# Second routed FFN of a macaron block: two token groups, rows scattered into expert slabs, 62 tiles instead of 47

## The chip, the cores and the metric

One core of a Trainium2 chip. The metric is the device time of one execution, in microseconds (us); the kernel before has a median of 578.79 us over 3 runs (578.08 to 579.34). The engines are TensorE (PE; its weight loads are shown as PEld), VectorE (DVE), ScalarE (ACT), GpSimd (POOL) and SyncE (SP), which only issues DMAs.

## The reference, cut to what matters

The input x has 4 batches of 512 tokens with 256 features (2048 tokens, 16 "token tiles" of 128).

```python
x = x + 0.5 * ffn(layernorm(x))        # FFN 1
x = x + attention(layernorm(x))        # 3 heads, per batch of 512 tokens
x = x + 0.5 * ffn(layernorm(x))        # FFN 2, the same weights

def ffn(x):                            # 16 experts, 2 per token, hidden size 128
    scores = sigmoid(x @ gate_w)
    selected = top_k(scores + expert_bias, 2)
    w = scores[selected] / sum(scores[selected])
    shared = (silu(x @ shared_gate) * (x @ shared_up)) @ shared_down
    routed = sum over the 2 experts e of w_e * ((silu(x @ G_e) * (x @ U_e)) @ D_e)
    return shared + routed
```

The attention is softmax(Q K^T / 16) V with the softmax over the query axis (each key's column is normalised), a mean over heads, an output product and a bias. All is float32; matrix products are done as three passes over values split in a high and a low part (`three_pass`).

## The kernel before, in words

Every engine has its own program, written out in Python in order; semaphores join them. The stages are: loading and splitting weights, with front 1 (layernorm, router, routing tables); FFN 1; attention; front 2; FFN 2; a tail with the shared expert and the combination.

**A routed FFN.** The 4096 (token, expert) pairs are sorted by expert. Each expert's rows start at a multiple of 128, so 4096/128 + 15 = 47 tiles of 128 rows always hold them (`SLOT_TILES`, `NI`). The routing part computes a slot for each pair (`choose`, `rank_tokens`, `slots`), then the inverse, a token number for each slot (`pick_tiles`, `pick_lanes`, `scale_tokens`, `index_tokens`), with which POOL gathers rows of normalised tokens from `xn_dram` by indirect DMA (`load`, L1580). The loop `ffn` (L518 PE, L851 ACT, L1300 DVE, L1694 SP) is a software pipeline of 47 + 4 steps: in step s PE transposes h of tile s-3 (L543), transposes the rows of tile s (L330), multiplies tile s-1 by gate and up weights and tile s-4 by the down weights (L324). ACT copies four results of PE a step (L862, L867, L878, L885), DVE makes the low parts and the product (L1307, L1311, L1316), SP stores the result in `y_dram` (L1703). PE reads the experts' weight addresses with one load of four registers per four tiles (L527).

**Attention** has 48 units (`units`: batch, head, key tile). Unit u computes scores, exponentials (ACT L979), their high and low part (ACT L988, POOL L1621), values (ACT L991, DVE L1428), and the product `mix` of unit u-2. Beside the units run side pieces, one `next()` of a generator at a time: `side_pieces` (between mix and values on PE) and `side_pieces_late` (at the end of the unit). The generators prepare the next batch (`attn_front`) and the normalised rows and router of FFN 2 for the batch before (`previous_front`, `prev_front`), whose rows SP stores in `xn_dram` (L1673). Batch 3 steps its FFN 2 generator twice a unit from its 7th unit on.

**Front 2** is what remains after the last `mix`: measure and normalise batch 3, transposes for the shared expert (`front_turn` PE L376, `front_hi` ACT L768, `front_lo` DVE L1072; 8 pairs of token tiles), the router of batch 3, the choice, ranks, slots, the inverse. `stay_busy` puts products on PE that nobody reads.

**The tail** after the loop: the shared expert by batch (`shared_gu`, `shared_silu`, `shared_mul`, `shared_hi`, `shared_lo`, `shared_y`, `shared_sink`), beside 32 indirect gathers of result rows by POOL (L1545, two per token tile, in bursts of 8, each burst after the landing of the one before), which DVE adds to x (`combine`, L1238), and 16 output DMAs (L1726).

## Time and profile before

| | us |
|---|---|
| median of 3 runs | 578.79 |
| the profiled execution, whole | 576.65 |
| its span, to which all rows below refer | 575.4 |
| attention ends | 409.4 |
| first product of FFN 2's loop | 442.56 |
| last result copied out of the loop | 522.02 |

Busy shares of the span: PE 81%, PEld 71%, DVE 59%, ACT 47%, POOL 44%. The page's 40 slices are 14.4 us each; PE stands at 8 or 9 tenths in most slices from the 6th to the 36th, at 6 or 7 in 12, 13, 16, 29, 31 and 32, and falls to 7, 4, 3, 2 in the last four. The line PEclk under it is the clock that PE was granted; it is at 8 or 9 tenths but for 7 in slices 3 to 5, 31, 38 and 39 and 6 in the last.

### The profile page before, as it was taken

To read this page: it belongs to the slowest core of one execution; us is meant where nothing else is said; L and a number is where in the kernel's file an instruction comes from. 1 tells how busy PE (TensorE), PEld (TensorE's weight loads), DVE (VectorE), ACT (ScalarE), POOL (GpSimd) and SP (SyncE) were. 2 spreads that over 40 slices of the span, in tenths; PEclk is the share of its full clock that TensorE was granted. 3 is DMA by queue.
4 is the path that set the end of the run, shared out by engine and by line. 5 is a ranking of instruction groups with operands and counts; after the bars stand their busy time and mean duration, and the time that the engine had idled before them with its cause. 6 is when DMAs were issued, how large, how long until landed. Compare 5 with 4: busy or idle time off the path is not lost.

```text
span 575.4 us, 9851 instructions
## 1 busy us (share of the span) xinstructions
PE 465.3 (81%) x3029; PEld 408.9 (71%) x3029; DVE 337.1 (59%) x925; ACT 272.6 (47%) x740; POOL 253.8 (44%) x259
## 2 busy tenths in 40 slices
PE   1675599999867997999899988999786799997432
PEld 0344488888655996898789977999755789886321
DVE  5478665555284666377538763635766566663554
ACT  4758266666424444345344544447333666662010
POOL 5356765553152542363237321422204555534655
PEclk9977799999989999999899999999897999999776
DMA  8642356466321100020001100003011455562444
GB/s 302 238 129 92 110 183 179 149 202 147 105 61 59 47 1 0 21 65 27 1 19 56 38 2 1 9 29 111 1 36 49 136 167 161 168 140 92 128 132 133
DMA packets 37808, 53.61 MB, mean 93 GB/s; under 512 B 5568, under 2 KB 30528, under 8 KB 37760
## 3 DMA queue, kind: packets, MB, share of 16 engines
q1 hardware_dynamic: 29760, 32.25, 16.8%
q0 software_dynamic: 7584, 20.72, 14.0%
q8 instruction: 27, 0.44, 0.3%
q14 instruction: 21, 0.17, 0.1%
q10 hardware_dynamic: 416, 0.02, 0.0%
HBM read 34.37 MB, written 18.61 MB: 92 GB/s over the span
## 4 chain that ended last, share of the span: by engine, by line
PE 57%; DVE 16%; issue 9%; ACT 6%; DMA 5%; POOL 5%; another core or an unknown queue 0%; SPq 0%; ACTq 0%; POOLq 0%; DVEq 0%
PE bank L324 47%; POOL late_pair L1545 4%; PE bank L330 3%; PE bank L543 2%; DMA late_pair<-y_dram,slot_i 2%; DMA raw<-xn_dram,gather_at 2%; PE bank L489 2%; DVE x_sb L1297 1%; DVE softmax_row L1418 1%; DMA x_sb<-in_x 1%; DVE e_sp L1307 1%; PE bank L376 1%; DVE v_sp L1428 1%; ACT v_sp L991 1%; DVE pick_lane L1180 1%
## 5 line engine op out<-in xcount | busy, mean ns | idle before, releaser
L1580 POOL DMA_INDIRECT raw<-xn_dram,gather_at x94 | 90.4, 962 | 87.3 <-PE bank L330 37.2
L1621 POOL TENSOR_TENSOR e_sp<-raw,e_sp 128x512 fp32r<-128x512 f32 x48 | 62.7, 1307 | 127.8 <-ACT e_sp L988 127.6
L324 PEld LDWEIGHTS bank<-v_sp,e_sp 128*128 128x128 f32 x576 | 75.5, 193 | 3.2 <-POOL e_sp L1621 0.3
L324 PE MATMUL bank<-v_sp,e_sp 128*128 128x256 f32 x576 | 77.7, 285 | 0.0
L324 PE MATMUL bank<-g_sp,xT 128*128 128x512 f32 x288 | 75.7, 398 | 1.4 <-DVE g_sp L1323 1.4
L979 ACT ACTIVATE raw<-bank,softmax_row 128x512 f32<-128x512 f32 x48 | 33.2, 692 | 58.0 <-DVE softmax_row L1418 57.9
L324 PEld LDWEIGHTS bank<-g_sp,xT 128*128 128x128 f32 x288 | 52.1, 190 | 11.0 <-DVE g_sp L1323 1.8
L1418 DVE TENSOR_REDUCE softmax_row<-bank 128x1 f32<-128x512 f32 x48 | 32.9, 686 | 38.0 <-PE bank L324 37.7
L324 PE MATMUL bank<-w_hi,e_sp 128*128 x188 | 50.5, 292 | 0.6 <-DVE e_sp L1307 0.6
L1307 DVE TENSOR_TENSOR e_sp<-bank,e_sp 128x128 fp32r<-128x128 f32 x94 | 27.4, 291 | 39.3 <-ACT e_sp L862 33.2
L324 PE MATMUL bank<-w_hi,v_sp 128*128 128x256 f32 x64 | 20.4, 397 | 35.5 <-DVE v_sp L1084 30.0
L324 PE MATMUL bank<-b_sp,xT 128*128 128x256 f32 x288 | 43.9, 288 | 3.7 <-DVE v_sp L1428 3.5
L324 PE MATMUL bank<-w_hi,xT 128*128 x188 | 45.4, 304 | 1.6 <-DVE xT L1311 1.6
L324 PE MATMUL bank<-w_hi,xt_late 128*128 x188 | 45.4, 304 | 1.4 <-DVE xt_late L1311 1.2
L1428 DVE SCALAR_TENSOR_TENSOR v_sp<-bank,softmax_row,v_sp 128x256 fp32r<-128x256 f32 x48 | 23.2, 484 | 34.9 <-ACT v_sp L991 34.3
L1545 POOL DMA_INDIRECT late_pair<-y_dram,slot_i x32 | 30.3, 948 | 29.6 <-DMA y_dram<-stage 13.3
L330 PE MATMUL bank<-ident,raw 128*128 128x128 f32 x212 | 41.2, 276 | 2.7 <-DMA raw<-xn_dram,gather_at 2.5
L885 ACT COPY stage<-bank 128x256 f32<-128x256 f32 x94 | 35.6, 378 | 15.9 <-PE bank L324 11.2
L324 PEld LDWEIGHTS bank<-w_hi,v_sp 128*128 128x128 f32 x64 | 16.0, 289 | 38.0 <-DVE v_sp L1084 31.9
L878 ACT ACTIVATE raw<-bank 128x128 f32<-128x128 f32 x94 | 26.7, 284 | 34.1 <-PE bank L324 29.1
L324 PEld LDWEIGHTS bank<-b_sp,xT 128*128 128x128 f32 x288 | 38.1, 190 | 6.2 <-DVE v_sp L1428 5.3
L1537 POOL DMA_INDIRECT stage<-y_dram,slot_i x32 | 31.4, 980 | 22.7 <-DMA y_dram<-stage 14.9
(204 smaller groups left out, 1086.7 us busy)
## 6 DMA issues: line engine op xcount, KB each, us to landing
y_dram<-stage SPq DMA_DIRECT2D x94, 128.0 KB
xn_dram<-xn_all SPq DMA_DIRECT2D x5, 512.0 KB, 4.3
stage<-in_w_pack SPq DMA_DIRECT2D x6, 384.0 KB, 5.4
raw<-in_w_pack SPq DMA_DIRECT2D x6, 384.0 KB, 3.1
x_sb<-in_x SPq DMA_DIRECT2D x4, 512.0 KB, 7.7
out<-x_sb SPq DMA_DIRECT2D x16, 128.0 KB
stage_more<-in_w_pack SPq DMA_DIRECT2D x5, 384.0 KB, 3.4
xn_dram<-raw SPq DMA_DIRECT2D x12, 128.0 KB, 1.7
```

The lines of the kernel that those rows point to most:

```text
L324: m = pe.matmul(dst, lhs[k][l], rhs[k][r], start=(first and k == 0 and i == 0), stop=(last and k == n - 1 and i == 2), skip_group_check=True)
L330: m = pe.transpose(dst[:, k * P:(k + 1) * P], src[:, k * P:(k + 1) * P], ident[:])
L878: act.activation(h_buf[:, g % 2, :], bank[GU_BANKS[g % 2]][:, 0:F], ACT.Silu).then_inc(s_silu, 1)
L885: act.copy(y_buf[:, d % Y_BUFS, :], bank[Y_BANKS[d % 2]][:, 0:H]).then_inc(s_y_copy, 1)
L979: act.activation(e32[:, i, :], bank[S_BANKS[i]][:], ACT.Exp, bias=row_max[:, i, :], accum_out=row_sum[:, i, :]).then_inc(s_exp, 1)
L1307: dve.tensor_tensor(ht_rows[:, v % 2, 1], bank[HT_BANK][:, 0:P], ht_rows[:, v % 2, 0].bitcast(F32), ALU.subtract).then_inc(s_hT_lo, 1)
L1418: dve.tensor_reduce(row_max[:, i, :], bank[S_BANKS[i]][:], AX, ALU.max, negate=True).then_inc(s_max, 1)
L1428: dve.scalar_tensor_tensor(out=v_sp[:, i, 1, :], in0=bank[V_BANK][:, 0:H], scalar=row_inv[:, i, :], in1=v_sp[:, i, 0, :].bitcast(F32), op0 ...
L1537: pool.indirect_dma_start(pair_buf[:, n % PAIRS, :], None, y_dram, at).then_inc(s_pair[n % PAIRS], 16)
L1545: pool.indirect_dma_start(late_pair[:, n, :], None, y_dram, at).then_inc(s_late[n % LATE_SEMS], 16)
L1580: pool.indirect_dma_start(row_buf[:, n % ROWS, :], None, xn_dram, bass.IndirectOffsetOnAxis(ap=gather_at[:, n:n + 1], axis=0)).then_inc(s_ ...
L1621: pool.tensor_tensor(e_sp[:, i, 1, :], e32[:, i, :], e_sp[:, i, 0, :].bitcast(F32), ALU.subtract).then_inc(s_e_lo, 1)
```

## The change

FFN 2's tokens are cut in two groups: the 12 token tiles of batches 0 to 2, and the 4 of batch 3. Each group has its own tiles: 12 x 2 + 15 = 39 and 4 x 2 + 15 = 23, together 62. The last two `mix` products of attention stand directly ahead of the loop, and `stay_busy` is gone.

Rows are no longer gathered through an inverse index. A DRAM tensor `slab_dram` has a fixed slab of rows for each expert; POOL scatters each normalised token tile into it twice (one indirect DMA per chosen expert, `slab_row`), and SP loads a tile's 128 rows with a plain DMA at an address from a register (`load_row`). Two groups of 16 DMAs of 128 KB (`clear_rest`) write zeros behind the last row of each expert. `pick_tiles`, `pick_lanes`, `scale_tokens` and `index_tokens` are used by FFN 1 alone.

The choice, ranks and slab addresses of a batch are made in attention's side pieces; batch 3 steps its generator twice a unit from its 5th unit on. The side sigmoid of batches 0 to 2 becomes an Exp on ACT with an addition and a reciprocal on DVE.

All of front 2 that needs batch 3, and the shared expert's transposes, are now side pieces of FFN 2's loop (`late_front`). The first 18 combinations are side pieces as well, from step 48 on, and POOL gathers from step 43 on into 8 places in place of 32.

The constants, and where attention's side pieces of batch 3 start:

```diff
+    LATE_T = (B - 1) * TB
+    LATE_TILES = (LATE_T * TOPK + E - 1, TB * TOPK + E - 1)
+    SPLIT_TILE = LATE_TILES[0]
+    TILES = (NI, sum(LATE_TILES))
+    STEPS = tuple(n + LAG for n in TILES)
+    LATE_PLACES = 8
+    PAIRS_FROM = 44
+    COMBINE_FROM = 48
+    EARLY_COMBINED = 9
...
-            if b == B - 1 and u % PER_BATCH >= PER_BATCH // 2:
+            if b == B - 1 and u % PER_BATCH >= PER_BATCH // 3:
                 next(ffn_side[b], None)
```

PE after attention's units:

```diff
             for w in MIXED_LATER:
-                if w == U - 1:
-                    front_turn(1, 0)
-                    front_turn(1, 1)
                 mix(w)
 
-            for n in range(2, FRONT_PAIRS - BATCH_PAIRS):
-                front_turn(1, n)
-            pe.wait_ge(s_mix_add, NT)
-            stay_busy(6)
...
-            ffn(1, lambda s: None)
+            late_side = late_front()
+            ffn(1, lambda s: next(late_side, None))
```

By steps of the loop, the side pieces are these. PE: 6 and 8 `front_turn` of batch 3, 10 `front_router`, 11 `turn_scores`, 14 `rank_again`, 16 `pack_table`, then six `front_turn`, one in three steps. ACT: 6 and 8 `front_hi`, 10 sigmoid (with its table, and Silu's table behind it), 13 `keep_score`, then six `front_hi`. DVE: 2 `measure`, 4 and 5 two `norm_rows` each, 7 and 9 `front_lo`, 12 and 13 `choose`, 14 `slab_rows`, 15 `tile_table`, 17 `write_table`, 18 `pair_slots`, 19 `routing_weights`, then six `front_lo`, from 48 one combination a step. SP: 3, 5 and 7 a reload of 512 KB of `xn_dram`, 16 `clear_rest(True)`.

DVE's side pieces in attention, the end of a batch's generator, and what they call. A piece that stands between two `yield`s is done in one go:

```diff
+                run(choose(1, (b - 1) * TB, b * TB))
+                yield
+                slab_rows(b - 1)
+                row_again((b - 1) * TB)
+                yield
+                row_again((b - 1) * TB + 1)
+                yield
                 if b == B - 1:
-                    yield from choose(1, 0, SPLIT_AT)
+                    row_again(b * TB - 2)
+                    tile_table(False)
+                    yield
+                    row_again(b * TB - 1)
+                    yield
+                    write_table(False)
+                    yield
+                    pair_slots(False)
+                    yield
+                    routing_weights(1, 0, LATE_T)
+                    yield
...
+            def row_again(t):
...
+                dve.wait_ge(s_slab[t % 2], 16 * TOPK * (t // 2))
+                norm_rows(xn_late[t % 2], t).then_inc(s_again, 1)
...
+            def tile_table(late):
+                first = SLAB_LATE if late else 0
+                dve.tensor_copy(zero_at[0:1, :], slab_to[0:1, :]).then_inc(s_zero_at, 1)
+                chained(dve.scalar_tensor_tensor(out=rounded[:, 1:], in0=slab_to[:], scalar=(P - 1) / 2.0 - first,
+                                                 in1=slab_at[:], op0=ALU.add, op1=ALU.subtract))
...
+                dve.scalar_tensor_tensor(out=tile_of[:, 1:2], in0=tile_of[:, 0:1], scalar=float(SLAB // P),
+                                         in1=tile_of[:, 3:4], op0=ALU.mult, op1=ALU.add).then_inc(s_counted, 1)
```

PE's at the same places:

```diff
+                yield
+                rank_again(b - 1)
+                yield
+                yield
                 if b == B - 1:
-                    yield from choose(b * TB)
+                    yield
+                    pack_table(False)
...
+            def pack_table(late):
+                pe.wait_ge(s_counted, 2 + late)
```

POOL scatters, and gathers results into 8 places:

```diff
+            def slab_row(t):
+                if t % TB == 0:
+                    pool.wait_ge(s_addr, t // TB + 1)
+                if t < LATE_T:
+                    pool.wait_ge(s_again, t + 1)
+                src, done = (xn_late[t % 2], s_slab[t % 2]) if t < LATE_T else (xn_all[:, t, :], s_slab_late)
+                for k in range(TOPK):
+                    pool.indirect_dma_start(slab_dram, bass.IndirectOffsetOnAxis(
+                        ap=addr_i[:, k, t:t + 1].bitcast(U32), axis=0), src, None).then_inc(done, 16)
...
+                    slab_row(b * TB - 1)
+                    pool.wait_ge(s_comb, NT * TOPK)
+                    pool.memset(zero_rows, 0.0).then_inc(s_zeros, 1)
...
+                        if n >= LATE_PLACES:
+                            pool.wait_ge(s_comb, NT * TOPK + n - LATE_PLACES + 1)
+                        if PAIRS_FROM + n < TILES[1]:
+                            pool.wait_ge(s_xt, BASE[1] + PAIRS_FROM + n)
```

SP, which in step s loads rows up to tile s + 3, waits for the result of tile s - 4 and stores it:

```diff
+            def load_row(n, rows):
...
+                if i == 0:
+                    sp.wait_ge(s_zero, 16 * E * (1 + late))
+                    sp.wait_ge(s_experts, 2 + late)
+                if i % PER_LOAD == 0:
+                    at = TABLE[late][1] + i
+                    _, rows["at"] = nc.values_load_multi_w_load_instructions(
+                        table[0:1, at:at + PER_LOAD], engines=[mybir.EngineType.SP], min_val=0,
+                        max_val=E * SLAB - P, skip_runtime_bounds_check_because=IN_SLAB)
+                if n >= ROWS:
+                    sp.wait_ge(s_xt, BASE[1] + n - ROWS + 1)
+                sp.dma_start(row_buf[1][:, n % ROWS, :], slab_dram[bass.ds(rows["at"][i % PER_LOAD], P), :]).then_inc(
+                    s_row_late[n % ROWS], 16)
+
+            def clear_rest(late):
+                sp.wait_ge(s_zero_at, 1 + late)
+                sp.wait_ge(s_zeros, 1)
+                for e in range(E):
+                    if e % PER_LOAD == 0:
+                        _, at = nc.values_load_multi_w_load_instructions(
+                            zero_at[0:1, e:e + PER_LOAD], engines=[mybir.EngineType.SP], min_val=0,
+                            max_val=E * SLAB - P, skip_runtime_bounds_check_because=IN_SLAB)
+                    sp.dma_start(slab_dram[bass.ds(at[e % PER_LOAD], P), :], zero_rows).then_inc(s_zero, 16)
```

The tail on DVE now combines token tiles 9 to 15 alone, with batch b's `shared_sink` ahead of batch b+1's `shared_lo`:

```diff
+            combine(1, EARLY_COMBINED)
+            shared_lo(1, 0)
+            shared_mul(1, 1)
+            combine(1, EARLY_COMBINED + 1)
+            shared_sink(1, 0)
+            shared_lo(1, 1)
...
+            combine(1, LATE_T + 2)
+            shared_sink(1, 3)
+            combine(1, LATE_T + 3)
```

## Rows read from the trace of the kernel before

**Rows 1.** Busy time by stage: start:end, length, then engines, clock, DMA share, GB/s.

```profile
382.00:409.37 27.37, 27.34 (x191) 25.26 (x190) 13.41 (x62) 16.16 (x33) 7.75 (x6) 1.00 0.19 64
409.37:442.56 33.19, 23.22 (x133) 17.12 (x132) 22.85 (x66) 11.94 (x29) 4.80 (x5) 0.79 0.09 27
442.56:522.02 79.46, 72.14 (x560) 66.74 (x560) 44.92 (x140) 50.76 (x187) 40.84 (x44) 1.00 0.54 149
522.02:575.40 53.38, 22.24 (x96) 18.53 (x96) 25.23 (x48) 4.41 (x8) 30.34 (x32) 0.76 0.40 123
```

**Rows 2.** Timeline behind attention: start us, us, engine, line, operation, tiles, count.

```profile
409.61 1.41 DVE L1337 TENSOR_TENSOR x_sb<-x_sb,bank 128x256 f32<-128x256 f32 x4
```

**Rows 3.** Instructions of two PE lines: duration ns min/median/max, first and last start us.

```profile
L543 PE MATMUL bank<-ident,raw x47: 270/272/303, 444.3 to 519.9; 128*128 128x128 f32 x47
...
L527 PEldq TENSOR_LOAD <-top_at x24: 327/331/521, 65.4 to 513.6; - x24
```

**Rows 4.** Timeline of two steps in FFN 2's loop, PE and DVE.

```profile
500.08 0.27 PE L543 MATMUL bank<-ident,raw 128*128 128x128 f32 x1
...
500.86 0.29 DVE L1307 TENSOR_TENSOR e_sp<-bank,e_sp 128x128 fp32r<-128x128 f32 x1 [0.34 <-issue]
...
501.48 0.27 PE L543 MATMUL bank<-ident,raw 128*128 128x128 f32 x1
```

**Rows 5.** Timeline of front 2: operations on PE that move into the loop.

```profile
406.61 1.04 PE L376 MATMUL bank<-ident,xn_all 128*128 128x128 f32 x8
...
421.16 1.57 PE L324 MATMUL bank<-xT,gate_sp 128*16 128x512 f32 x6 [0.70 <-DVE xT L1072]
```

**Rows 6.** Timeline of front 2: ACT.

```profile
422.77 0.59 ACT L789 ACTIVATE route<-bank 16x512 f32<-16x512 f32 x1 [1.08 <-PE bank L324]
...
424.63 1.28 ACT L1004 ACT_TABLE_LOAD   x1
...
425.93 0.20 ACT L1004 ACTIVATE softmax_row<-columns 128x1 f32<-128x1 f32 x1
```

**Rows 7.** Timeline of front 2: DVE.

```profile
416.75 1.38 DVE L1042 TENSOR_SCALAR xn_all<-x_sb,moments,rstd 128x256 f32<-128x256 f32 x4
...
438.49 0.17 DVE L1204 TENSOR_TENSOR total_w<-weight 128x16 f32<-128x16 f32 x1
```

**Rows 8.** Busy time while batch 3 is chosen (columns as in rows 1).

```profile
424.09:426.13 2.04, 1.55 (x6) 0.94 (x6) 1.89 (x16) 1.70 (x3) 0.00 (x0) 1.00 0.00 0
```

**Rows 9.** SP's issues, ns min/median/max; the time to landing is that of the 128 KB stores of L1673.

```profile
L1703 SPq DMA_DIRECT2D y_dram<-stage x94: 319/320/628, 73.3 to 522.0; - x94
...
L1692 SPq DMA_DIRECT2D stage_more<-in_fc_t x1: 497/497/497, 116.4 to 116.4; - x1
...
DMA to landing us min/median/max: 1.7/1.7/3.6
```

**Rows 10.** Chain that ended last, a gather in FFN 1 beside two 256 KB loads.

```profile
138.65 7.23 DMA raw<-xn_dram,gather_at
```

**Rows 11.** Timeline of attention's last units: one POOL subtraction, one mix.

```profile
396.27 1.29 POOL L1621 TENSOR_TENSOR e_sp<-raw,e_sp 128x512 fp32r<-128x512 f32 x1 [3.82 <-ACT e_sp L988]
...
399.48 1.59 PE L324 MATMUL bank<-v_sp,e_sp 128*128 128x256 f32 x12
```

**Rows 12.** Timeline of the tail: the first two gathers.

```profile
524.57 0.95 POOL L1545 DMA_INDIRECT late_pair<-y_dram,slot_i  x1 [13.27 <-DMA y_dram<-stage]
525.83 0.95 POOL L1545 DMA_INDIRECT late_pair<-y_dram,slot_i  x1 [0.30 <-issue]
```

**Rows 13.** Chain that ended last: its last gather and combination.

```profile
570.28 2.81 DMA late_pair<-y_dram,slot_i
...
573.12 0.48 DVE x_sb L1238
```

**Rows 14.** Busy time in the tail: gate and up products of two batches, down product of one.

```profile
522.27:528.00 5.73, 5.73 (x24) 4.39 (x24) 1.19 (x2) 1.67 (x3) 2.82 (x3) 1.00 0.24 75
529.71:531.40 1.69, 1.69 (x13) 1.69 (x14) 0.82 (x2) 0.00 (x0) 1.39 (x2) 1.00 0.37 104
```

More of the change, by code:

```diff
@@ L58, in macaron @@
     AT_LOADS = -(-SLOT_TILES // PER_LOAD)
+    IN_SLAB = "a place in a slab: the expert is at most E - 1 and a rank at most the tokens routed so far"
     BOUNDED = "tile_expert is a count of is_le over E ends, held at E - 1 by a min"
@@ L899, in previous_front, with late_front @@
                 yield from prev_front(b - 1)
-                if b == B - 1:
-                    yield from choose()
+                for _ in range(3 if b < B - 1 else 8):
+                    yield
+            def late_front():
+                for _ in range(6):
+                    yield
+                front_hi(1, FRONT_PAIRS - 2)
+                yield
+                yield
+                front_hi(1, FRONT_PAIRS - 1)
+                yield
+                yield
+                front_sigmoid(1, B - 1)
+                act.wait_ge(s_inv_sum, U)
+                act.wait_ge(s_warm, 2)
+                act.activation(row_sum[:, 0], minus_half[:, 0:1], ACT.Silu).then_inc(s_warm, 1)
+                yield
+                yield
+                yield
+                keep_score(1)
+                yield
+                for _ in range(5):
+                    yield
+                for n in range(FRONT_PAIRS - BATCH_PAIRS):
+                    yield
+                    front_hi(1, n)
+                    yield
+                    yield
             act.wait_ge(s_zeroed, 1)
@@ L1345, in previous_front @@
             def previous_front(b):
-                yield
-                yield
+                for t in range((b - 1) * TB - 2, (b - 1) * TB):
+                    if t >= 0:
+                        row_again(t)
+                    yield
                 measure(b - 1)
@@ new lines, in late_front @@
+            def late_front():
+                yield
+                yield
+                measure(B - 1)
+                yield
+                yield
+                dve.wait_ge(s_rstd[2], B)
+                dve.wait_ge(s_v, U)
+                for t in range(LATE_T, NT):
+                    norm_rows(xn_all[:, t, :], t).then_inc(s_row_norm, 1)
+                    if t % 2 == 1:
+                        yield
+                yield
+                front_lo(1, FRONT_PAIRS - 2)
+                yield
+                yield
+                front_lo(1, FRONT_PAIRS - 1)
+                yield
+                yield
+                yield
+                late_choice = choose(1, LATE_T, NT)
+                next(late_choice)
+                next(late_choice)
+                yield
+                run(late_choice)
+                yield
+                slab_rows(B - 1)
+                yield
+                tile_table(True)
+                yield
+                yield
+                write_table(True)
+                yield
+                pair_slots(True)
+                yield
+                routing_weights(1, LATE_T, NT)
+                yield
+                for n in range(FRONT_PAIRS - BATCH_PAIRS):
+                    yield
+                    front_lo(1, n)
+                    yield
+                    yield
+                while True:
+                    yield
@@ L1626, in pool_program @@
             norm_scale(2, B - 1)
-            ffn(1, lambda s: None)
-            run(tail2())
-        load_from, load_to = [], []
-        done = 0
-        for s in range(STEPS):
-            load_from.append(done)
-            limit = min(s + 4, NI)
-            done = max(done, limit)
-            load_to.append(done)
+            pool.wait_ge(s_row_norm, NT + TB)
+            for t in range(LATE_T, NT):
+                slab_row(t)
+            for t in range(NT):
+                gather_pair(1, t)
         def sp_program():
@@ L1715, in previous_front, with late_front @@
                 yield from prev_front(b - 1)
+                yield
+                yield
+                yield
                 if b == B - 1:
[L1717 removed]
+                    yield
+                    clear_rest(False)
+                    yield
+                    yield
+                    yield
+                    yield
+            def late_front(s):
+                if s in (3, 5, 7):
+                    reload_batch((s - 3) // 2)
+                if s == 16:
+                    clear_rest(True)
             def tail2():
```

601 lines of the change are left out of this document (358 added, 243 removed).

## The prediction

> **What bounds the kernel now.** I read the page's slices first: PE is near its limit through attention and both FFN loops, and low in slices 29 to 31 and in the last four. Busy time by stage puts numbers on it [rows 1]. Attention's last 27.4 us: PE busy 27.3, nothing to win but by less work. Front 2, 33.2 us from attention's end to the first product of the loop: PE busy 23.2, much of it `stay_busy`, clock 0.79; DVE is busy 22.9 in one chain of routing steps. The loop, 79.5 us: PE 72.1, ACT 50.8, DVE 44.9, so PE sets its pace. The tail, 53.4 us: PE 22.2 at clock 0.76, while POOL issues 32 gathers. The chain that ended last goes through POOL there: a gather takes 0.95 us and the next starts 1.25 us after it [rows 12], bursts wait for landings, and the last one lands 2.8 us later, before the last combination of 0.48 [rows 13].
>
> Attention ends at 409.4, the loop's products run from 442.6 to the last result at 522.0, the span to 575.4 [rows 1]. The sum is made on these four stages.
>
> **Stage 1, attention: +6.2 us.** PE gets four small rank and pack groups and loses nothing it waited for: +1.0. The rest is batch 3's end, where the generator goes two pieces a unit and a unit takes about 3.5 us. `slab_row` puts four indirect DMAs (5 us by the pace of [rows 12]) beside each POOL subtraction of 1.29 [rows 11], so POOL owes more than a unit's time for two units. In the trace the subtraction of unit 44 ended at 397.6 and `mix` took its result at 399.5 [rows 11]: 1.9 us of cover. More: in unit 44 DVE must do `row_again(10)`, which waits for the scatters of tile 8. With POOL free for them at 392.1 they are issued by 394.3 and land 2.8 us after the second began [rows 13]: 396.1. Behind it stand a normalisation (1.38 for four, 0.4 each [rows 7]) and `tile_table`, eleven small chained operations of 0.17 plus some 0.04 between them [rows 7]: 2.4 us, until 398.9. But PE's `pack_table(False)` is in the same piece, and PE reaches it at 395.0, with all of the next unit's products queued behind it: 4.0 us of stall. POOL's backlog is worked off meanwhile. Then `pair_slots` (about 1.9) and `routing_weights` (about 2.1) delay the maxima of units 46 and 47 by 1.2 us. 1.0 + 4.0 + 1.2 = 6.2. Bounds: 1.0 (all waits covered) and 12 (POOL's 5 us comes on top).
>
> **Stage 2, front 2: 33.2 becomes 2.9, a gain of 30.3.** The first tile needs DVE's four additions (1.41 [rows 2]), a transpose, ACT's and DVE's copies: 2.3 us behind the last `mix`. Its row must be there too: the first zero writes wait for POOL's memset behind its last scatter (404.2), take SP 16 x 0.32 [rows 9] and 4 x 0.33 for register loads [rows 3], 6.4 us, land, and only then is row 0 issued: +0.6. First product at 409.4 + 6.2 + 2.9 = 418.5. Bounds 2.3 and 7.
>
> **Stage 3, the loop: 79.5 becomes 125, a loss of 45.5.** A clean step is 1.40 us [rows 4], the mean from first to last transpose 75.6 / 46 = 1.64 [rows 3]. 15 tiles more at 1.60: +24.0 (21.0 at 1.40, 24.7 at 1.64). Front 2's work comes inside:
> - PE itself: 8 `front_turn` at 0.52 [rows 5], router 1.57 [rows 5], scores, ranks and pack about 1.0: 6.8. PE sets the pace, so it counts whole.
> - ACT's Silu table of 1.28 at the start, of which 0.8 shows; at step 10 sigmoid's and Silu's table, 2 x 1.28, with 0.59 and 0.20 for the functions [rows 6]; the first load lies beside PE's router, so 1.6 beyond it.
> - DVE: between two operations of a step it has 0.34 us idle, and the next step's transpose waits for the second after 0.33 more [rows 4]; a piece up to 0.67 is hidden, what is above it stops PE. `measure` 1.9 costs 1.2, the normalisations 0.3, `choose` 1.8 [rows 8] 1.1, `slab_rows` 1.3 costs 0.7, `tile_table` 2.3 costs 1.6: 4.9. The 18 combinations of 0.48 [rows 13] are under the limit: 0.5.
> - SP: at step 16 the zero writes hold it for 5.1 + 1.3 us, then row 20 needs a register load, an issue and 1.7 us to land [rows 9], with 2 MB in front of it: about 10.3 us after the result that SP waited for, where PE wants it after 4.5. 5.8, and in this hole `write_table`, `pair_slots` and `routing_weights` vanish. SP's three reloads of 512 KB put a row behind them; in FFN 1 a gather took 7.2 us beside 512 KB [rows 10] against three steps of 4.7 here. I take 1.0 (0 to 7).
>
> 6.8 + 2.4 + 5.4 + 5.8 + 1.0 = 21.4, with the 24.0 45.4. Bounds of the 21.4: 9 (PE's own and 2 for SP) and 43 (DVE's 26 us of added work and ACT's stand beside nothing).
>
> **Stage 4, the tail: 53.4 becomes 27.3, a gain of 26.1.** 24 of 32 gathers are issued before the loop's end or just after it: one a step from step 43, 1.25 against 1.6 us. The last eight wait for all results and start 2.55 us after the last copy [rows 12], which gives 2.6 + 7 x 1.25 + 2.8 + 0.5 + 1.8 (the output's flight) = 16.4. No longer the longest. The shared expert is: gate and up 5.73 for two batches, down 1.7 for one [rows 14]; four batches 18.3. Between them PE waits for `shared_hi` and `shared_lo`: 0.25, three times 0.6, and 2.6 for batch 3, whose `shared_lo` stands behind two combinations; then the last sink, two combinations and the output, 3.9. Together 26.9, and 0.4 for holes at half clock: before, the clock was 0.76 here [rows 1]. Bounds 25 and 33.
>
> **Sum.** 6.2 - 30.3 + 45.4 - 26.1 = -4.8; a little of the stages' joints (POOL's gathers among rows and stores, 3 x 128 KB a step, against 2 before) I set at +0.7. -4.1 of 575.4. The profiled execution took 576.65 for that span, so it would be 572.5; it lies 2.1 under the median of 578.79, and in the median's terms the forecast is 574.7.
>
> **A rule weighed.** ACT's table load ended at 425.91 and the next function began at 425.93 [rows 6]: nothing is left behind a load. The Trainium skill (ScalarE: Activation LUTs, section "What ACT_TABLE_LOAD costs") has 1.38 us of draining with each switch. By it three switches in the loop would cost 4.1 us more, 578.8 in all. The row speaks against it here.
>
> **The rivals.**
> 1. The holes take more: the pieces fall where PE waits already (per four tiles it loses about 0.8 us beside the register load), `pack_table` finds its table ready. Stage 1 +3, stage 3's 21.4 becomes 15: 574.7 - 3.2 - 6.4 = 565. For it: DVE is idle 34.5 of 79.5 us in the loop [rows 1]. Against: a step's chain leaves only 0.67 in one place.
> 2. SP's zero writes are dearer, and it ends slower. Place: 16 in front of row 0, 16 in front of row 20, both on the path. Price: issues of the same queue took 0.32 to 0.50 us [rows 9], and with addresses from registers they may take 0.55: 32 x 0.23 = 7.4 us, 582.1. It decides from 0.45 us an issue on (32 x 0.13 = 4.2), where the whole gain is gone. Against: row 0's issues are partly early.
> 3. DVE's chains cost their full length: four pieces above 1 us lose no 0.67, +2.7, and the maxima in attention another 1.3: 578.7, no change.
> 4. A drain behind each table load: 3 x 1.38, 578.8, no change; as a mechanism the row denies it.
> That the change doesn't do what it says would show as row 39 late: its scatters (8 x 1.25) come after step 14, 20 steps ahead. I give it nothing of its own.
>
> **Chances.** Forecast 0.40, holes 0.22, SP 0.25, DVE's chains 0.10, drain 0.03. A measurement of this kernel tells 0.2% (1.2 us) from no change: faster is below 577.6, slower above 580.0. The forecast's own range is 570 to 579; 0.34 of its 0.40 are faster, 0.04 no change, 0.02 slower. With 0.22 of the holes and 0.02 of the last two faster is 0.58; no change 0.04 + 0.06 = 0.10; slower 0.32. Range 564 to 587: from rival 1 to somewhat above rival 2, for attention's upper bound.
>
> **What would show it.** Attention's end near 415.6, with PE waiting about 4 us in `pack_table`; the loop's first product near 418.5; one hole of 5 to 6 us before the transpose of tile 20, its releaser a DMA into row_buf; loop's end near 544; in the tail no wait of DVE for late gathers, PE's products of four batches nearly in a row. Wrong if the loop's mean step away from the side pieces is over 1.7 us (DMA or SP bound), if row 0 comes later than 419, or if the tail is again paced by POOL.

## The result, and the profile after

The changed kernel is slower: a median of 604.39 us over 4 runs (597.78 to 611.39) against 579.07 over 4 runs of the kernel before (578.08 to 580.92), a ratio of 1.040 (95% interval 1.030 to 1.049). The forecast was 574.7, the range 564 to 587. The ratio is taken over the runs in the machine's faster state, to which one of the four (611.39) doesn't belong, so it isn't quite the quotient of the medians; later ratios are meant likewise. The profiled execution took 597.78 us with a span of 596.5; all rows of this section refer to it. It is the fastest of the four, so the stages below account for its span and not for the 6.6 us between it and the median.

Busy time by stage, first the last 27.4 us of attention, then the gap, the loop and the tail, with the columns of [rows 1]:

```profile
405.74:433.11 27.37, 19.65 (x125) 17.55 (x125) 15.17 (x49) 8.32 (x18) 14.53 (x14) 0.88 0.34 116
433.11:436.99 3.88, 1.37 (x10) 0.70 (x8) 1.84 (x5) 0.49 (x2) 0.00 (x0) 1.00 0.50 142
436.99:568.80 131.81, 108.87 (x791) 99.74 (x791) 77.64 (x270) 77.74 (x261) 31.70 (x33) 0.92 0.58 178
568.80:596.48 27.68, 19.46 (x96) 15.72 (x96) 16.37 (x30) 4.41 (x8) 8.17 (x8) 0.93 0.42 128
```

| | before | forecast | measured |
|---|---|---|---|
| attention ends | 409.4 | 415.6 | 433.1 |
| gap to the first product | 33.2 | 2.9 | 3.9 |
| loop | 79.5 | 125 | 131.8 |
| tail | 53.4 | 27.3 | 27.7 |

Two of four stages are as forecast: the gap gives 29.3 us (forecast 30.3), and the tail 25.7 (26.1). The loop costs 6.8 more than forecast, and attention 17.5 more. That is 24.3 of the 25.2 us by which the span misses its forecast of 571.3. In the last 27.4 us of attention, PE was busy 27.34 of 27.37 before; now it is busy 19.65, at a granted clock of 0.88 in place of 1.00.

The five largest entries of what PE waited for from batch 1 on to attention's end (line waited at, releaser: us in total, times, longest):

```profile
PE bank L504 <- issue: 7.9, 2, 4.0
PE bank L524 <- DVE tile_of L1293: 5.0, 1, 5.0
PE bank L357 <- POOL e_sp L1874: 4.9, 2, 3.9
PE bank L387 <- issue: 3.5, 4, 1.4
PE bank L357 <- DVE v_sp L1682: 2.1, 2, 1.7
```

L504 is `rank_again`, L524 `pack_table`, L357 every three-pass product. The kernel before had 3.5 at its router products too, and beside it 2.3 for xT and 0.4 for v. The three larger ones of the new are shown below. The rank's (PE, then DVE; start, duration, operation, and in brackets the idle time ahead of it and its releaser):

```profile
289.23 0.21 PE L504 MATMUL bank<-choice,before 128*128 128x64 f16 x1 [3.96 <-issue]
289.43 4.35 PE L357 MATMUL bank<-xT,a_sp 128*128 128x512 f32 x12
```

```profile
284.15 0.18 DVE L1224 TENSOR_SCALAR route<-route 128x64 f32<-128x64 f32 x1
...
286.77 0.23 DVE L1249 TENSOR_TENSOR choice<-route 128x64 f16<-128x64 f32 x1
286.91 0.68 DVE L1672 TENSOR_REDUCE softmax_row<-bank 128x1 f32<-128x512 f32 x1
288.70 0.42 DVE L1468 TENSOR_TENSOR xT<-bank,xT 128x256 fp32r<-128x256 f32 x1 [1.11 <-ACT xT L930]
```

The choice was ready at 287.0, but the rank product waits for its PSUM bank too (`wait_bank7` in the kernel): the last transpose of xT, the transposed input of the next batch, lies in it until DVE's subtraction L1468 has read it, which ended at 289.12. DVE gets there late, as 2.8 us of choice stand ahead of the row maximum (L1672), ACT's exponential and ACT's copy, in this order. Behind the hole twelve products of 128x512 took 4.35 us at a granted clock of 0.67, in the other such place 5.22 at 0.54; undisturbed ones take 2.91 at 1.00. The pack's wait, in batch 3, and POOL in batch 2:

```profile
414.62 0.42 PE L524 MATMUL bank<-ident,tile_of 128*1 128x40 f32 x4 [5.02 <-DVE tile_of L1293]
414.98 2.93 PE L357 MATMUL bank<-g_sp,xT 128*128 128x512 f32 x6
```

```profile
304.38 1.32 POOL L1874 TENSOR_TENSOR e_sp<-raw,e_sp 128x512 fp32r<-128x512 f32 x1
305.87 1.01 POOL L1800 DMA_INDIRECT slab_dram<-raw,lane  x1 [0.17 <-issue]
307.19 0.98 POOL L1800 DMA_INDIRECT slab_dram<-raw,lane  x1 [0.30 <-issue]
308.47 0.98 POOL L1782 DMA_INDIRECT stage<-y_dram,slot_i  x1 [0.30 <-issue]
309.75 0.96 POOL L1782 DMA_INDIRECT stage<-y_dram,slot_i  x1 [0.30 <-issue]
310.74 1.30 POOL L1874 TENSOR_TENSOR e_sp<-raw,e_sp 128x512 fp32r<-128x512 f32 x1
```

Two scatters (L1800), two gathers for FFN 1's combination (L1782) and a subtraction make 6.36 us a unit, against PE's 5. Three units of it are in a row, and behind them `mix`, which needs POOL's subtraction, waited 3.91 us until 318.42.

In the loop, SP's second row of zero writes and row 20 behind it (SP, then PE; "x16" is 16 issues in a row):

```profile
470.32 13.81 SPq L1968 DMA_DIRECT2D slab_dram<-stage  x16
484.72 0.35 SPq L1957 DMA_DIRECT2D stage<-slab_dram  x1
```

```profile
480.21 0.45 PE L608 MATMUL bank<-ident,raw 128*128 128x128 f32 x1 [4.63 <-DVE e_sp L1488]
486.79 0.64 PE L363 MATMUL bank<-ident,stage 128*128 128x128 f32 x2 [3.57 <-DMA stage<-slab_dram]
```

From the transpose of row 17 (470.06) to that of row 21 (490.21) it is 20.1 us; four undisturbed steps a little later take 6.3. There are two long waits in it, the forecast had one. The second, for row 20, is the forecast's. The first is behind row 18: PE waited 4.63 for DVE, and DVE for ACT. Away from the side pieces' first half, from row 21 to row 47, a step takes 1.58 on average, where the forecast had 1.60 for each added tile.

### The profile page after: what moved, and what is told of

It reads as the page before. It is cut to its first block and busy times, and to the rows that moved or that the text cites. A ratio compares the mean times of both kernels' runs of the same rounds, so it can differ in the third digit from the quotient of the medians.

```text
span 596.5 us, 10777 instructions
## 1 busy us (share of the span) xinstructions
PE 485.2 (81%) x3143; PEld 428.2 (72%) x3143; DVE 359.0 (60%) x1044; ACT 285.0 (48%) x785; POOL 241.8 (41%) x245
## 3 DMA queue, kind: packets, MB, share of 16 engines
q0 software_dynamic: 6864, 18.75, 11.3%
## 5 line engine op out<-in xcount | busy, mean ns | idle before, releaser
L357 PE MATMUL bank<-v_sp,e_sp 128*128 128x256 f32 x576 | 79.2, 288 | 4.9 <-POOL e_sp L1874 4.9
L357 PEld LDWEIGHTS bank<-v_sp,e_sp 128*128 128x128 f32 x576 | 76.1, 195 | 9.1 <-POOL e_sp L1874 6.3
L357 PE MATMUL bank<-g_sp,xT 128*128 128x512 f32 x288 | 77.8, 406 | 1.4 <-DVE g_sp L1504 1.4
L1092 ACT ACTIVATE raw<-bank,softmax_row 128x512 f32<-128x512 f32 x48 | 33.2, 692 | 75.5 <-DVE softmax_row L1672 75.5
L357 PE MATMUL bank<-w_hi,xt_late 128*128 x248 | 62.5, 314 | 2.9 <-issue 2.9
L357 PE MATMUL bank<-w_hi,e_sp 128*128 x218 | 61.3, 302 | 0.6 <-DVE e_sp L1488 0.3
L357 PEld LDWEIGHTS bank<-g_sp,xT 128*128 128x128 f32 x288 | 53.2, 194 | 11.5 <-DVE g_sp L1504 1.8
L1827 POOL DMA_INDIRECT raw<-xn_dram,gather_at x47 | 46.7, 993 | 33.3 <-PE bank L363 21.5
L1488 DVE TENSOR_TENSOR e_sp<-bank,e_sp 128x128 fp32r<-128x128 f32 x109 | 31.5, 289 | 41.2 <-ACT e_sp L946 35.5
L1672 DVE TENSOR_REDUCE softmax_row<-bank 128x1 f32<-128x512 f32 x48 | 33.0, 687 | 36.5 <-PE bank L357 32.8
L963 ACT ACTIVATE raw<-bank 128x128 f32<-128x128 f32 x109 | 30.7, 282 | 49.5 <-PE bank L357 39.3
L1497 DVE TENSOR_TENSOR raw<-raw,bank 128x128 f32<-128x128 f32 x109 | 31.1, 285 | 35.1 <-ACT raw L963 28.0
L357 PE MATMUL bank<-b_sp,xT 128*128 128x256 f32 x288 | 44.3, 290 | 5.3 <-DVE v_sp L1682 5.2
L357 PEld LDWEIGHTS bank<-w_hi,xt_late 128*128 128x128 f32 x248 | 44.6, 198 | 5.5 <-issue 4.2
L608 PE MATMUL bank<-ident,raw 128*128 128x128 f32 x109 | 31.8, 292 | 19.6 <-DVE e_sp L1488 15.0
L357 PE MATMUL bank<-w_hi,xT 128*128 x188 | 47.0, 311 | 0.5 <-DVE xT L1492 0.5
L357 PEld LDWEIGHTS bank<-w_hi,e_sp 128*128 128x128 f32 x218 | 43.3, 199 | 2.9 <-issue 1.8
L357 PEld LDWEIGHTS bank<-b_sp,xT 128*128 128x128 f32 x288 | 38.6, 192 | 8.1 <-DVE v_sp L1682 7.1
L357 PE MATMUL bank<-xT,a_sp 128*128 128x512 f32 x144 | 39.0, 424 | 2.9 <-DVE xT L1446 1.7
```

The lines of the kernel that those rows point to most:

```text
L357: m = pe.matmul(dst, lhs[k][l], rhs[k][r], start=(first and k == 0 and i == 0), stop=(last and k == n - 1 and i == 2), skip_group_check=True)
L608: pe.transpose(bank[HT_BANK][:, 0:P], h_buf[:, v % 2, :], ident[:]).then_inc(s_hT, 1)
L963: act.activation(h_buf[:, g % 2, :], bank[GU_BANKS[g % 2]][:, 0:F], ACT.Silu).then_inc(s_silu, 1)
L1092: act.activation(e32[:, i, :], bank[S_BANKS[i]][:], ACT.Exp, bias=row_max[:, i, :], accum_out=row_sum[:, i, :]).then_inc(s_exp, 1)
L1488: dve.tensor_tensor(ht_rows[:, v % 2, 1], bank[HT_BANK][:, 0:P], ht_rows[:, v % 2, 0].bitcast(F32), ALU.subtract).then_inc(s_hT_lo, 1)
L1497: dve.tensor_tensor(h_buf[:, g % 2, :], h_buf[:, g % 2, :], bank[GU_BANKS[g % 2]][:, F:GU], ALU.mult).then_inc(s_act, 1)
```

## The experiments

The kernel before took 578.4 us in the first series below and 563.5 to 564.2 in the others, one of them on the same chip as the first. So times are compared within a series, or as ratios; where a stage of one series stands beside one of another, the text says so. Runs marked "1 run" have one time alone, and the changed kernel's own times span 13.6 us: from them only the stages of the trace are used. "Batch 1, 2, 3" is the time from one batch's first addition (DVE, L1337 before, L1518 after) to the next one's.

**First series: one suspect each.** Spread zeros:

```diff
-                if s == 16:
-                    clear_rest(True)
+                if 16 <= s < 16 + E:
+                    clear_rest(True, [s - 16])
```

> One edit: the second 16 zero writes (one of 128 KB for each expert) are issued one a step, in steps 16 to 31, not all in step 16. Theory A, the burst is the hole: between the transposes of row 16 and row 20 the changed kernel takes 20.1 us where four clean steps of 1.6 take 6.4; spread, it should be 7 to 9, the loop 131.8 minus 11 to 13 (about 120), the profiled time about 585 against 597.8. Rival B, the hole is made by DVE's routing pieces (table, slots, weights) and POOL's eight scatters, which stay where they are: at least 12 us of the 20 remain and the time stays above 592.

Measured: 599.72 us (4 runs), ratio 1.038 (1.032 to 1.044), so the clock time didn't tell it from the changed kernel's 1.040. The loop, from its first row to its last result, was 129.6 us against 133.6. Rows 17 to 21 took 14.7 in place of 20.1. By the numbers that is rival B (at least 12, and above 592 us): the wait for row 20 is gone, but the step behind row 18 stayed, at 7.3, and in it ACT's Silu came 1.6 us after the product that it needs. Neither theory had that delay; the third series returns to it. Spreading had a price too: PE now waited for other rows, 0.2 to 1.3 us each (rows 25, 28 and 32), so of the 5.4 us only 4.0 show in the loop.

Ranks one unit later:

```diff
-                rank_again(b - 1)
-                yield
+                if b == B - 1:
+                    rank_again(b - 1)
+                yield
+                if b < B - 1:
+                    rank_again(b - 1)
                 yield
```

> One edit: in attention's batches 1 and 2 the rank products, the slab addresses and the repeated rows that need them come one piece later (unit 12 of the batch in place of 11), behind the last xT turn's release. Theory A, PE's two waits of 3.96 us are for the bank that the last turn holds and that DVE frees only behind the choice (2.8 us), and the half clock behind each hole costs 1.4 and 2.2 us more: both waits go, batches 1 and 2 together fall from 133.4 to about 122. As a scatter moves into the units with gathers, POOL may give back 1 to 3 us in batch 2. Rival B, the choice holds the row maxima anyway: the idle time shows up ahead of mix or scores in the same unit and the two batches lose less than 4 us.

Measured: 611.04 us (1 run). PE's wait didn't go, it moved to the next product that needs xT:

```profile
294.70 4.60 PE L357 MATMUL bank<-xT,a_sp 128*128 128x512 f32 x12 [3.91 <-DVE xT L1471]
```

Batch 1 was 64.4 (64.4 to 64.9 in the other kernels of the series), batch 2 74.7 against 71.3: with one more scatter in a unit with gathers, PE's waits for POOL there rose from 3.9 to 6.0. So theory A was wrong in what to move. It should be the choice that has to go behind the last turn, while the rank only waits beside it; the second series tests that.

Scatters of tiles 2 to 7 out of the units with gathers (the numbers are the pieces of batch 1, 2 and 3 in which each tile is scattered):

```diff
+        ROWS_AT = {1: {11: [0], 12: [1]}, 2: {10: [2], 11: [3], 12: [4]}, 3: {1: [5], 2: [6], 3: [7], 11: [8], ...}}
```

> One edit: tiles 2 to 7 are scattered later (tiles 2 and 3 in batch 2's units 10 and 11 in place of units 1 and 2, where POOL also gathers for FFN 1; tiles 4 to 7 shift with them). Theory A, POOL's pace of 6.3 us a unit (two scatters, two gathers of 1.27 each and a subtraction of 1.3) against PE's 5 is what makes mix wait 3.9 us in batch 2, with 1.6 us of half clock behind it: batch 2 falls from 70.4 to about 65, no wait on POOL above 1 us. Rival B, it is the normalisation of batch 2 (POOL's rstd, behind the gathers) that is late, or the wait comes back where the scatters now are: batch 2 stays above 68.

Measured: 599.6 us (1 run), batch 2 65.5 us against 71.3 in the kernel with spread zeros, forecast 65. Batch 3 took 60.1 against 59.2. No POOL is left in what PE waited for in batch 2:

```profile
PE bank L508 <- issue: 4.3, 1, 4.3
PE bank L391 <- issue: 1.7, 2, 1.4
PE bank L367 <- DVE raw L1150: 0.4, 1, 0.4
```

Pack two pieces later, DVE's copy of the table behind slots and weights:

```diff
+                    yield
+                    yield
                     pack_table(False)
...
-                    write_table(False)
-                    yield
                     pair_slots(False)
                     yield
                     routing_weights(1, 0, LATE_T)
                     yield
+                    write_table(False)
+                    yield
```

> One edit: in batch 3 PE's pack products come two pieces later, and DVE's copy of the table behind the slots and the weights. Theory A, PE's wait of 5.02 us is for DVE's chain behind the late scatter of tile 8 and for nothing else: it goes with its 1.4 us of half clock, batch 3 falls from 58.9 to 52 or 53. Rival B, DVE's chain (address, row, 11 small operations) delays the row maxima as much: PE waits as long for scores or v, batch 3 stays above 56. The first row of the loop may come some tenths later.

Measured: 608.09 us (1 run). Batch 3 was 57.5 (59.2 in the kernel with spread zeros): rival B. Pack's 5.0 is gone, and in its place, from 378.4 on:

```profile
PE bank L363 <- DMA stage<-slab_dram: 5.2, 1, 5.2
PE bank L357 <- DVE v_sp L1682: 3.4, 2, 2.5
PE bank L357 <- issue: 2.4, 1, 2.4
PE bank L357 <- POOL e_sp L1874: 1.7, 2, 1.0
```

The clock of batch 3 rose to 1.00 (0.91), but DVE's chain is paid for at v, and the first row of the loop waited 5.2 us. That wait isn't for the later table: it was written at 429.0, while SP was still issuing the first burst of zero writes.

```profile
428.79 0.19 DVE L1305 TENSOR_SCALAR table<-bank 1x40 int32<-1x40 f32 x1
```

```profile
425.73 10.83 SPq L1968 DMA_DIRECT2D slab_dram<-stage  x16
439.13 3.89 SPq L1957 DMA_DIRECT2D stage<-slab_dram  x6
```

Row 0 was issued 2.6 us behind the burst's end, against 2.0 in the changed kernel, where most of it lay beside attention.

**Second series: parts together.** Scatters and gathers one a step, beside the spread zeros:

```diff
                 for k in range(TOPK):
+                    if t >= LATE_T:
+                        pool.wait_ge(s_xt, BASE[1] + 16 + (t - LATE_T) * TOPK + k)
...
-    PAIRS_FROM = 44
+    PAIRS_FROM = 46
```

> Beside the edit of the spread zero writes, POOL's eight scatters of batch 3 are issued one a step (steps 16 to 23) in place of eight in a row, and the early gathers of the combination one a step from step 46 in place of four in a row at their start. With the zeros spread a step of 7.3 us was left, in which ACT's Silu started 1.6 us and its result copy 2.7 us after PE's products had ended, until POOL's row of scatters was over; a step of 3.9 to 4.0 us stood in the same way behind the four gathers. Theory A, a row of indirect DMAs issued back to back holds up what PE tells the others: the 7.3 becomes below 3 and the 3.9 below 2.5, the loop about 122 us in place of 129.6. Rival B, the holes have another cause at these steps (instruction fetch, DVE's pieces): both stay within 1 us of what they are.

Measured: 575.8 us (1 run; the kernel before 563.66). The step of 7.3 became 1.4, the one of 3.9 became 2.4, the loop, from its first row, 113.6 us. That looked like theory A, but the machine had changed too, and the third series shows the step of 1.4 without the edit as well.

Attention reordered (the diff is shown against the kernel with the moved scatters): a plan for the scatters much like that one's, the choice of batches 1 and 2 in unit 11 of the batch and the ranks in unit 12, `tile_table(False)` ahead of `row_again(10)`:

```diff
-                run(choose(1, (b - 1) * TB, b * TB))
+                if b == B - 1:
+                    run(choose(1, (b - 1) * TB, b * TB))
                 again(10)
                 yield
                 if b == B - 1:
                     slab_rows(b - 1)
+                else:
+                    run(choose(1, (b - 1) * TB, b * TB))
```

> Attention alone is reordered. Batches 1 and 2: the choice on DVE comes behind the last xT turn (unit 11 of the batch in place of 10), ranks and addresses in unit 12; rows 1 to 7 are scattered in units without gathers. Batch 3: the tile table goes ahead of the repeated row that waits for a scatter, and pack one piece later. Theory A, the ranks' wait of 4.0 is DVE's choice standing ahead of the last turn's subtraction (moved alone, the wait turned up as 3.9 for xT ahead of the next make_g): both waits fall to about 1.2, as in the kernel before, POOL's 3.9 is gone, pack's 5.0 is below 1.5. With the clock the three batches take 61, 61 and 54 us in place of 64.5, 71 and 59; the time is some 15 to 18 us under the changed kernel's. Rival B, DVE's work is what counts wherever it stands: the waits move to the row maxima and v, and less than 7 us are won.

Measured: 577.14 us (1 run). Batches 60.1, 63.5 and 58.4; forecast 61, 61 and 54. The rank's waits are gone, and the wait for xT, 2.6 in two places, is what the kernel before had (2.3). Neither the rank alone (64.4) nor the scatters alone (64.6) had moved batch 1, so there it is the choice. Theory A holds for batches 1 and 2 but for 2.5 us in batch 2, and not for batch 3:

```profile
PE bank L367 <- DMA stage<-slab_dram: 5.2, 1, 5.2
PE bank L361 <- DVE v_sp L1698: 3.2, 3, 1.7
PE bank L361 <- POOL e_sp L1895: 3.2, 3, 1.6
```

Pack is down to 0.5, but v and POOL took its place, and the loop's first row came 5.2 us late behind the zero burst. The second burst is left as it was here, so within this series it can be read against the kernel with spread zeros and paced scatters: rows 17 to 21 take 16.2 us with it and 7.3 there.

Both parts together:

> Both: attention reordered, zeros, scatters and gathers spread. If the two parts add up, attention ends at about 418 and the loop takes about 122 us, with 3.4 for the gap and 27.7 for the tail: 571 of span, 572 to 574 in the profile, some 0.5 to 1% faster than the kernel before. If the rivals hold in part: attention at 425 and the loop 127, 585, slower than before.

Measured: 570.31 us (4 runs), ratio 1.014 (1.008 to 1.019), where 0.5 to 1% faster than the kernel before was forecast. The loop, from its first row, was 115.8 us, six less than forecast, but attention ended at 421 (418), and row 0 came 5.0 us late. The kernel before was faster in this series too (563.66 against 578.4), which a forecast in microseconds from the first series didn't have.

**Third series: controls.** The changed kernel again, the kernel before again, and the paced scatters with the zeros in one burst:

> The changed kernel itself, unedited, as a yardstick on the chip of this series: the kernel before took 578.4 us in the first series and 563.7 in the second, so stage times of kernels of different series can't be subtracted. Theory A, the chip only scales the stages: attention 190 to 192 us over the three batches, the loop near 130 with the steps of 7.8, 6.3 and 4.0 us in it, time 4% above the kernel before. Rival B, the steps of 7.8 and 4.0 belong to the first chip and not to the kernel: the loop is 120 to 125.

> The kernel before itself, unedited, to read its stages on the chip of this series. If the chip only scales: attention's three batches 166 us, front 2 33, the loop 79 to 80, the tail 53, each within 1%. If the difference of 15 us between the chips of the two series sits in one stage, it is one of those with DMA in it (FFN 1, the tail), and attention stays at 166.

> The changed kernel with one edit: POOL's eight scatters of batch 3 one a step; the 16 zero writes stay in one burst at step 16. Theory A (a row of indirect DMAs holds up PE's signals): of the steps 17 to 21, 24 us in the changed kernel, the 7.8 goes to below 3 and the wait for row 20 (6 to 8 us) stays. Rival B (the zero writes do both): the steps are what they are in the unedited kernel of this series, within 1 us.

Measured: the changed kernel 584.28 us (4 runs), ratio 1.033 (1.025 to 1.041); the paced one 582.05 (1 run); its edit has the scatters' part alone, the gathers stay as they were. Stages of the kernel before, then of the changed one, in this series: batches 1 to 3, the gap, the loop from its first row, the tail.

```profile
240.70:300.30 59.60, 56.61 (x359) 51.22 (x358) 37.89 (x90) 26.93 (x62) 25.47 (x22) 0.97 0.09 27
300.30:360.30 60.00, 56.66 (x358) 50.87 (x357) 37.87 (x89) 26.81 (x62) 23.49 (x20) 0.97 0.08 23
360.30:408.60 48.30, 48.30 (x329) 44.38 (x327) 25.55 (x96) 26.87 (x57) 15.18 (x12) 1.00 0.13 45
408.60:438.26 29.66, 19.98 (x127) 14.23 (x126) 22.01 (x65) 11.44 (x27) 3.50 (x4) 0.88 0.08 24
438.26:511.89 73.63, 70.10 (x565) 66.68 (x563) 46.40 (x141) 52.07 (x188) 42.02 (x45) 1.00 0.61 164
511.89:565.00 53.11, 22.88 (x96) 18.99 (x96) 25.24 (x48) 4.42 (x9) 30.26 (x32) 0.74 0.41 123
```

```profile
241.40:306.30 64.90, 59.13 (x365) 53.11 (x364) 42.66 (x114) 27.01 (x63) 27.88 (x25) 0.92 0.10 30
306.30:377.60 71.30, 61.67 (x360) 54.72 (x360) 42.98 (x116) 27.00 (x63) 33.16 (x31) 0.88 0.12 38
377.60:436.40 58.80, 50.05 (x326) 44.95 (x325) 33.87 (x108) 23.53 (x53) 27.02 (x25) 0.94 0.21 71
436.40:438.10 1.70, 0.31 (x4) 0.11 (x2) 1.42 (x4) 0.00 (x0) 0.00 (x0) 1.00 0.39 102
438.10:557.98 119.88, 103.36 (x795) 95.78 (x795) 79.31 (x271) 78.79 (x262) 29.73 (x31) 0.96 0.64 195
557.98:585.80 27.82, 19.61 (x96) 15.81 (x96) 16.38 (x30) 4.41 (x9) 9.85 (x10) 0.93 0.47 141
```

What to see: attention and tail are within 2.7 us of the first series, the loop, from its first row, is shorter: 73.6 us for 81.3 before, 119.9 for 133.6 after. The unedited kernel has no step of 7.8 at row 18 here (1.4), and its step behind the gathers is 3.1; with the scatters paced they are 1.4 and 3.4. So this is rival B: the long step belongs to the first series and not to the kernel alone. A row of eight indirect DMAs doesn't make it by itself; whether it did together with whatever was different in the first series, no run tests. The gathers' step was 2.4 with the gathers paced, on another chip, which isn't enough to say that pacing them helps. What is left of the hole is the zero burst:

```profile
471.39 9.88 SPq L1968 DMA_DIRECT2D slab_dram<-stage  x16
481.85 0.35 SPq L1957 DMA_DIRECT2D stage<-slab_dram  x1
```

```profile
483.98 0.69 PE L363 MATMUL bank<-ident,stage 128*128 128x128 f32 x2 [7.72 <-DMA stage<-slab_dram]
487.44 0.63 PE L363 MATMUL bank<-ident,stage 128*128 128x128 f32 x2
```

Row 20 was issued 0.6 us behind the burst, and PE's transpose of it (483.98) came 2.1 us after that. Rows 17 to 21: 16.2 us with the burst, 16.0 with it and paced scatters. In the second series they are 16.2 with the burst and 7.3 without: the burst costs 8.8 us.

Thinner: batch 3's pieces go two a unit from its third unit on, zero rows filled and written earlier, `choose` and `tile_table` cut in the loop:

```diff
-            if b == B - 1 and u % PER_BATCH >= PER_BATCH // 3:
+            if b == B - 1 and u % PER_BATCH >= PER_BATCH // 6:
...
+                next(late_choice)
+                yield
                 run(late_choice)
                 yield
                 slab_rows(B - 1)
                 yield
-                tile_table(True)
+                late_table = tile_table_parts(True)
+                next(late_table)
+                yield
+                run(late_table)
```

> The reordered kernel (attention and loop) with three more edits: batch 3's side pieces go two a unit from its third unit on in place of the fifth, the zero rows are filled ahead of the last scatters and the first zero writes follow the tile table at once (row 0 came 5.0 us late behind them), and DVE's choice and tile table in the loop are cut in two pieces each. Theory A: row 0's wait falls below 1.5 us and the loop loses 2 to 3 us more, 6 to 7 us under the reordered kernel, which was 1.4% above the kernel before: a ratio of 1.000 to 1.004. Rival B: the denser units ahead give part back in mix's waits for POOL, ratio 1.008 or more.

Measured: 559.16 us (4 runs; the kernel before 563.5), ratio 0.989 (0.981 to 0.996). The forecast had 1.000 to 1.004. This beats both kernels, by little: the interval ends just below 1. Against the two parts together (an earlier series, another chip) row 0's wait of 5.0 is gone, the time from the first addition behind attention to the loop's last result is 114.2 us in place of 121.4, and batch 3 is 56.8 in place of 58.4. The three edits weren't timed one by one.

**Fourth series: what is left in batch 3.** `pair_slots(False)` and `routing_weights(1, 0, LATE_T)` in steps 0 and 1 of the loop:

> The thinner kernel with DVE's slots and weights of the first three batches (some 5 us of DVE work in batch 3's units 9 to 11) moved into steps 0 and 1 of the loop. Batch 3 still takes 56.8 us against 48.3 in the kernel before, with 4.9 of PE's waits on v_sp, 1.9 on POOL. Theory A, DVE's side work in batch 3 is what is left of attention's loss: batch 3 falls by 3 to 5 us, and the loop's first steps lose 2 to 3. Rival B, what is left is POOL's (scatters beside the subtractions): batch 3 falls by less than 1.5 and the time does not fall.

> The thinner kernel again, unedited, with more rounds: it stood at 0.989 of the kernel before with an interval of 0.981 to 0.996. If that holds beyond one chip, 0.985 to 0.995 here; if it was the chip (the changed kernel itself stood at 1.038 on one and at 1.033 on another), up to 1.000.

Measured: the thinner kernel again 0.989 (0.986 to 0.993; medians 560.17 and 564.19 us), 5 rounds; with weights in the loop 0.994 (0.991 to 0.997; 560.45 us). Batch 3 fell from 56.7 to 53.5 (3.2: theory A), and the time from its end to the loop's last result rose from 111.9 to 115.1 (3.2). In these two traces the same DVE work costs PE the same in either place, and the clock time shows no gain. Of the 5.2 us between 53.5 and the 48.3 of before, 5.0 stand in PE's waits in batch 3: for POOL (1.9), the choice (1.3), v (1.1) and ACT's scores (0.7). What each would give alone wasn't tried. In the loop's first steps PE waited 3.1 for the copies of transposed rows, against 0.9 in the thinner kernel.

## Why the prediction was wrong

**Attention, +6.2 forecast, +27.1 measured** (195.0 against 167.9 us for batches 1 to 3 in the third series, where they lost 5.3, 11.3 and 10.5; 192.3 against 166.3 in the first traces, with 2.2 won ahead of batch 1). This is the step that failed, at three terms:
- "PE gets four small rank and pack groups and loses nothing it waited for: +1.0." Batches 1 and 2 were given nothing else. Each lost 4.0 to a wait, for a bank that DVE frees behind the choice, and 1.4 to 2.3 to the lower clock behind it. I had counted that the choice was ready in time, not who else holds the product's bank, and which of DVE's own links stand behind 2.8 us of new work. Moving the choice gave batch 1 back: 60.1, against 64.4 to 64.9 wherever it stayed and 59.6 in the kernel before.
- POOL was reckoned for batch 3 only, where there are no gathers. In batch 2 scatters and gathers share three units, 6.36 us a unit against 5. The size of the loss (the wait of 3.9, and with the clock 5.8 of batch 2) was shown by moving the scatters alone.
- In batch 3 pack's 4.0 was 5.0, from the cause given: rank, address, a row that waits 2.16 for its scatter, the table. But I stopped at that wait. DVE's busy time in the batch rose from 25.6 to 33.9 us and POOL's from 15.2 to 27.0, where the batch had taken 48.3. With pack's wait removed alone, 1.7 us were won, and PE waited at v instead; with attention reordered, the batch still took 58.4. That it is the amount of side work and not one late link is shown in part: 3.2 us left the batch when 5.8 us of DVE's busy time did.

**The gap, 2.9 forecast, 3.9 measured**: near, with row 0 late by 1.6 behind the first zero burst, where I had 0.6. The burst held SP for 9.3 us and not for 6.4, and attention's end covered most of it, 11.6 us from the burst's start. With both parts together it covered only 9.7, of a burst that took 10.6, and the wait was 5.0.

**The loop, +45.5 forecast; +52.3 in the first trace, +46.3 in the third series.** The mis-sized term is the second zero burst: "16 x 0.32" and 1.3, 6.4 us of SP and a hole of 5.8. The single issues were as assumed (0.33 in the median of 32), but 16 in a row took 13.8 and 9.9 us, 0.86 and 0.62 an issue with all that lies between, and the hole was 8.8 (with the burst against without it, second series). The other terms come to 37.5 together in the third series, forecast 39.7; they weren't tested one by one. That is rival 2's mechanism, at a price above the 0.55 it had; I gave it 0.25, and its total of 582.1 hadn't the attention in it. Of the 6.0 us that the loop lost on top in the first trace, about 4 lie in rows 17 to 21 (20.1 against 16.2), where the step behind row 18 is, whose cause stays open; the other 2 weren't placed.

**The tail, -26.1 forecast, -25.7 and -25.3 measured**: right, down to its mechanism: ahead of three of the four `shared_y` PE waited 0.53, ahead of the last 2.69, where the forecast had about 0.6 and 2.6, and no gather held it.

**The signs of the forecast's list** did their work: attention's end at 433 and not 415.6 was the first number to look at, PE waited 5.0 at `pack_table`, and the loop's hole for row 20 was where it should be, with its releaser a DMA into the row buffer. The drain behind table loads (rival 4) isn't there: the three loads in the loop (437.26, 454.25 and 456.15, 1.28 each) have a function 0.02 us behind them.

## What to carry to other kernels

When side work is put into a stage that is already full, add it up by engine and unit first (POOL 6.36 against 5 would have stood there), and then ask for each new piece what of the same engine stands behind it in that unit. Removing one wait in such a stage proves little: two of the four single edits here only moved it, or most of it, and the kernel before was beaten only when order, load and the bursts were changed together. In this kernel a burst of DMA issues cost what the row of them held its engine, not 16 times one issue.

## What was not expected of the hardware

Sixteen writes of 128 KB from one queue, each issue 0.31 to 0.71 us in itself, held SP for 9.26, 13.81, 9.88 and 10.64 us in three traces; at 2 MB that is 227 to 152 GB/s. The loop moves 178 to 203 GB/s over its whole length. The traces show the time between the issues, not its cause.

```profile
L1968 SPq DMA_DIRECT2D slab_dram<-stage x32: 314/332/705, 421.5 to 483.8; - x32
```

In the changed kernel's first trace and the first series, five kernels, the step behind row 18 took 7.3 to 8.4 us. In it ACT's Silu started 3.8 us after PE's last product ahead of it had ended by its record (475.2 in the first trace):

```profile
478.99 0.28 ACT L963 ACTIVATE raw<-bank 128x128 f32<-128x128 f32 x1 [5.33 <-remote]
```

In the later series, on the same code, that step took 1.4. The kernel before was faster too, by 10.4 us between its two traces, 7.7 of them in the loop. It isn't the chip alone: the first and the fourth series ran on the same one, with 578.4 and 564.2 us for the kernel before. No run tells why. These kernels can only be compared when they are timed side by side.
